# Ranking score matmuls by ScalarE's queued work in the planner of a causal attention stage

## The chip, the cores and the metric

One NeuronCore of one Trainium2 chip runs the whole program in one launch. The metric is device time in microseconds, the median of several executions. The program has six stages one after the other; the change lies in the fifth, the second attention, and there in one host-side function that writes down the order of the instructions before the kernel is built.

## The reference, cut to what matters

The program is a "macaron" of feed-forward and attention layers on 2048 tokens of width 256, each with a layer norm ahead and a residual behind:

```python
x = x + 0.5 * _L0_ffn_ref(_layernorm(x), ...)
x = x + _L0_attn_ref(_layernorm(x), ...)      # latent attention, 16 heads
x = x + 0.5 * _L0_ffn_ref(_layernorm(x), ...)
x = x + 0.5 * _L1_ffn_ref(_layernorm(x), ...)
x = x + _L1_attn_ref(_layernorm(x), ...)      # the stage of the change
x = x + 0.5 * _L1_ffn_ref(_layernorm(x), ...)
```

The second attention, with 16 heads of width 16, all 2048 tokens in one causal sequence:

```python
q, k, v = _rope(proj(Wq)), _rope(proj(Wk)), proj(Wv)
scores = jnp.einsum('bhsd,bhtd->bhst', q, k) * attn_scale
scores = jnp.where(causal, -jnp.inf, scores)
probs = jax.nn.softmax(scores, axis=-1)
out = jnp.einsum('bhst,bhtd->bhsd', probs, v)
return out.transpose(0, 2, 1, 3).reshape(B, S, E) @ Wo.T
```

The softmax is taken with the true maximum of each row, and all matmuls work on 32-bit data.

## The kernel before, in words

**Tiling.** Queries come in 4 chunks of 512 tokens and heads in 4 groups of 4; a pair (chunk j, group g) is a *unit*. There are 16 units, `UNITS` (L1327), in chunk order 0, 3, 2, 1, four units each. A unit of chunk j looks at 4(j+1) *key tiles* of 128 keys; one key tile of one unit is a *step* (160 in all). Each step has four *scores* matmuls, one for each head.

**The five kinds of TensorE work** (`attention_heads`, the TensorE block around L1800 to L1863), with what follows each on another engine:

- *maxima*: the scores of a piece of a unit with queries on the partitions, two heads at a time, into one of two PSUM `slot`s of 1024 columns. VectorE reduces the slot to row maxima (L1875, L1881) and so frees it. A unit of chunk j has 2(3+4j) such jobs: 6, 14, 22 or 30. In each half of a unit the first is a *triangle*: two bf16 matmuls with the mask on all 128 rows of the array (L1812) and eight small ones (L1816). All others are L1824. Head h uses the upper or lower 64 rows of the array, so two matmuls of different halves can run side by side.
- *turn*: when all maxima of a unit are known, VectorE combines and negates them (L1887 to L1894, event *shift*), TensorE turns them (L1831), VectorE copies them (L1900), and SyncE's queue places them beside the queries by DMA (L1790).
- *scores*: key tile against the unit's 512 queries (fewer on the diagonal: 384, 256 or 128), shift included, into one of three PSUM banks (L1841). ScalarE takes the exponential into `probs` (L1922) and so frees the bank. On the diagonal GpSimd clears what lies ahead (L1769).
- *values*: the four heads of a step against V, in four column groups of 32 (L1854; 8 matmul instructions, the 32-bit data taking two passes each). It waits until the step's four exponentials are done. `probs` holds four steps, so scores may run at most four steps ahead of values.
- *finish*: after a unit's last values, ScalarE drains the output bank (L1929), TensorE turns it back (L1861), VectorE divides (L1905, L1907).

**What sets the order.** `attention_plan` is a greedy list scheduler with a model of its own. It keeps when each slot, bank, half of the array and engine will be free (`slot_free`, `bank_free`, `half_free`, `scalar_at`, `vector_at`), works out for each kind of work that may come next the time `at` at which it could start, and takes the one with the lowest `at + PREFER[kind]`; ties go to the earlier `at`. `SWITCH` is charged where the array's layout changes (scores and maxima share "rows", values is "columns", turn and finish are "whole"), `RESULT` from a matmul to its reader, `SIGNAL` from a reader to the next writer. The result is one fixed list for each engine, which the engine's block follows in order; every instruction still waits on its semaphores. So a change of `PREFER` changes no instruction, only the order on TensorE and, where two units or kinds cross, on the other engines.

The model's charges, from the code: an exponential 0.09 + width/1200 us, a scores matmul 0.06 + width/2400, values 0.12 + width/600, a triangle 0.85, a reduction 0.1 for each part + 2 x width/960, and 4.0 us from a turn's copy until the unit's scores can start.

Before, the order comes out as a repeated pattern. Written with V for values, s for scores, m for maxima, T for turn and F for finish, the list begins `mmmmmmmmTmmmmmsssmssTsssmsmsssmsss...`; after the first four units comes `VmFmmmmmmmmmmmmmmmmmmmTmmmmmsssmss`, then long runs of `VsssmmsVsssmmsVsssmms`, and after the last maxima `VsssVsssVsss`.

Of the kernel before, what the change touches and what calls it, by code (L numbers as in the profile page):

```python
# [1328 lines left out]
HEAD_COLUMNS = D1 + 1  # L1329
PLACED = 3 * D1  # L1330
SWITCH, RESULT, SIGNAL = 0.08, 0.25, 0.12
PREFER = {"turn": -0.3, "finish": -0.3, "scores": -0.05, "maxima": 0.0, "values": 0.1}


def maxima_jobs(j):
# [21 lines left out]
def attention_plan():  # L1357
# [13 lines left out]
    mode, slot_free, bank_free = None, [0.0, 0.0], [0.0] * 3  # L1371
    step_ready, value_done = [], []
    jobs = scored = valued = unit = job = 0
    shift_at, turned, finish_at, finished, drained_at, ready_at = {}, set(), {}, set(), {-1: 0.0}, {}
    query_ready = {n: 0.0 if n < NG else 12.0 for n in range(2 * NG)}

    def wide_start(ready, to):
        return max(ready, *half_free, issue) + (0.0 if mode == to else SWITCH)

    def narrow_start(ready, halves):  # L1380
        return max(ready, issue, *(half_free[i] for i in halves)) + (0.0 if mode == "rows" else SWITCH)

    while scored < GROUP * len(steps) or valued < len(steps) or len(finished) < units:
        choices = []
        free = slot_free[jobs % 2]
        for n in sorted(shift_at):
            if n not in turned:
                choices.append((wide_start(max(free, shift_at[n]), "whole"), PREFER["turn"], "turn", n))
        for n in sorted(finish_at):
            if n not in finished:  # L1390
                choices.append((wide_start(max(free, finish_at[n]), "whole"), PREFER["finish"], "finish", n))
        if unit in query_ready:
            choices.append((narrow_start(max(free, query_ready[unit]), (0, 1)), PREFER["maxima"], "maxima", unit))
        if scored < GROUP * len(steps):
            step, h = divmod(scored, GROUP)
            n, kt = steps[step]
            if n in ready_at and (step < PROB_STEPS or len(value_done) > step - PROB_STEPS):
                choices.append((narrow_start(max(bank_free[scored % 3], ready_at[n]), (h % 2,)), PREFER["scores"], "scores", n))
        if valued < len(step_ready):
            n, kt = steps[valued]  # L1400
            if n - 1 in drained_at:
                choices.append((wide_start(max(step_ready[valued], drained_at[n - 1] if kt == 0 else 0.0), "columns"),
                                PREFER["values"], "values", n))
        _, at, kind, n = min((c[0] + c[1], c[0], c[2], c[3]) for c in choices)
# [29 lines left out]
        elif kind == "scores":  # L1434
            step, h = divmod(scored, GROUP)
# [7 lines left out]
            scalar_at = start + 0.09 + width / 1200  # L1443
# [11 lines left out]
        elif kind == "values":  # L1455
# [5 lines left out]
            if kt == key_tiles(j) - 1:  # L1461
                scalar_at = max(scalar_at, end + RESULT)
# [248 lines left out]
def attention_heads(core, scratch, first_query, key, v_one, attended):  # L1711

    nc = core.nc
    plan = attention_plan()
    ring = {e[2]: e for e in plan["tensor"] if e[0] in ("maxima", "turn", "finish")}
    place = {(e[0], e[1]): e[2] for e in plan["tensor"] if e[0] in ("turn", "finish")}
# [284 lines left out]
```

How the kernel before makes its waits and increments, by code:

```python
    def __call__(self, instruction):  # L133
        instruction.then_inc(self.sem, 1)
        self.n += 1
        self.engine.wait_ge(self.sem, self.n)
# [26 lines left out]
    def vector(self, dve):  # L163
        dve.wait_ge(self.masks_loaded, 16)
        self.core.nc.vector.tensor_copy(self.core.masks[:], self.masks[:]).then_inc(self.masks_ready, 1)
# [19 lines left out]
    def vector(self, dve):  # L186
        for b in range(0, 2 * NCH, 2):
            dve.wait_ge(self.turned, b + 1)
            self.core.nc.vector.tensor_copy(self.place(b), self.banks[b % len(self.banks)][:]).then_inc(self.evac_dve, 1)
# [1 line left out]
    def scalar(self, act):  # L191
        for b in range(1, 2 * NCH, 2):
            act.wait_ge(self.turned, b + 1)
            self.core.nc.scalar.activation(self.place(b), self.banks[b % len(self.banks)][:], ACT.Copy).then_inc(self.evac_act, 1)
# [1 line left out]
    def tensor(self, pe):  # L196
        nc, n = self.core.nc, len(self.banks)
        for b in range(2 * NCH):
            c, d = divmod(b, ND)
            if self.source_ready is not None:
                pe.wait_ge(self.source_ready, TPC * (c + 1))
            if b >= n:
                pe.wait_ge(self.evac_act if b % 2 else self.evac_dve, (b - n) // 2 + 1)
            for i in range(TPC):
                last = nc.tensor.transpose(self.banks[b % n][:, i * P:(i + 1) * P],
                                           self.source[:, TPC * c + i, d * P:(d + 1) * P], self.core.ident)
            last.then_inc(self.turned, 1)
```

## Time and profile before

| | |
|---|---|
| median of 3 runs | 1953.37 us (1953.34 to 1963.35) |
| the profiled execution, its own time | 1954.15 us |
| its span, first to last instruction | 1952.4 us |
| TensorE busy | 1731.2 us, 89% |
| VectorE busy | 1529.0 us, 78% |
| ScalarE busy | 1179.7 us, 60% |
| GpSimd busy | 983.2 us, 50% |
| mean granted TensorE clock | 0.933 |

"Busy" is the union of the durations of an engine's instructions; matmuls are pipelined, so a busy TensorE need not be at its peak. Granted clock 1 is 2.4 GHz and 0.5 is 1.2 GHz; a value between is a stretch with both. The stage of the change runs from about 1432 to 1896 us of the span.

### The profile page before, as it was taken

How to read it: one execution, taken by the hardware profiler on the slowest of the kernel's cores; microseconds unless marked ns; L12 is line 12 of the kernel's file. 1: busy time of each engine (PE TensorE's matmuls, PEld its weight loads, DVE VectorE, ACT ScalarE, POOL GpSimd, SP SyncE). 2: the span in 40 equal slices, each digit the busy share in tenths (PEclk: the TensorE clock that was granted, in tenths of full speed). 3: DMA queues.
4: the chain of work that ended last, by engine and by line, in shares of the span. 5: the costliest groups of instructions: out<-in, count | busy, mean ns of one | idle time of the engine just before them, and what ended most of it. 6: DMA issues, size and time to landing. Idle time of an engine off the chain costs nothing. (4 is left out here: it accounts for less than half of the span.)

```text
span 1952.4 us, 27188 instructions
## 1 busy us (share of the span) xinstructions
PE 1731.2 (89%) x9368; PEld 1005.0 (51%) x9368; DVE 1529.0 (78%) x2236; ACT 1179.7 (60%) x2043; POOL 983.2 (50%) x820
## 2 busy tenths in 40 slices
PE   4667899999999999999999997557978999999996
PEld 3544555555555565565555653456644444444445
DVE  6763888998898888988889887776658888887716
ACT  1145787776876777777778774111323577777760
POOL 0004798897896988979879886011401000010110
PEclk8786999999999999999999999677968899999988
DMA  3200000000000000000000000111430200200001
GB/s 100 63 16 24 1 1 1 15 1 15 1 1 15 1 6 10 1 15 1 0 7 1 1 1 3 45 46 38 97 55 2 33 2 2 34 2 2 2 2 43
DMA packets 26697, 34.34 MB, mean 18 GB/s; under 512 B 5312, under 2 KB 19648, under 8 KB 26432
## 3 DMA queue, kind: packets, MB, share of 16 engines
q1 hardware_dynamic: 25360, 31.28, 6.7%
q8 instruction: 76, 1.25, 0.3%
q10 hardware_dynamic: 1200, 1.31, 0.2%
q14 instruction: 61, 0.50, 0.1%
HBM read 26.03 MB, written 6.29 MB: 17 GB/s over the span
## 5 line engine op out<-in xcount | busy, mean ns | idle before, releaser
L1208 POOL TENSOR_TENSOR lath_summed<-lath_summed,lath_held 128x512 f32<-128x512 f32 x392 | 524.8, 1339 | 54.4 <-ACT lath_held L1114 27.5
L1922 ACT ACTIVATE atth_probs<-atth_score 128x512 f32<-128x512 f32 (+3 forms) x640 | 293.3, 542 | 156.4 <-PE atth_score L1841 154.1
L1279 DVE TENSOR_TENSOR lath_held<-lath_held,lath_shift 128x1024 f32<-128x1024 f32 (+2 forms) x352 | 331.2, 968 | 24.6 <-PE lath_shift L1027 15.0
L1108 ACT ACTIVATE lath_held<-lath_score 128x1024 f32<-128x1024 f32 (+2 forms) x352 | 283.7, 828 | 105.1 <-DVE lath_largest L1232 51.5
L1881 DVE TENSOR_REDUCE atth_maxima<-atth_slot 128x2 f32<-128x1024 f32 (+3 forms) x288 | 285.9, 1041 | 53.5 <-PE atth_slot L1824 52.5
L1114 ACT ACTIVATE lath_held<-lath_held 128x1024 f32<-128x1024 f32 (+2 forms) x352 | 292.6, 861 | 48.7 <-DVE lath_held L1279 47.1
L1014 PE MATMUL lath_out<-lath_held,lat_latent 128*64 128x512 f32 (+1 forms) x1152 | 302.9, 591 | 8.0 <-ACT lath_held L1114 4.3
L998 PE MATMUL lath_score<-lath_query_hi,lat_key_hi 128*128 128x512 f32 x576 | 246.7, 428 | 22.8 <-ACT lath_held L1108 17.7
L1769 POOL TENSOR_SCALAR_AFFINE_SELECT atth_probs<-atth_probs 128x512 f32<-128x512 f32 x64 | 40.6, 635 | 433.9 <-ACT atth_probs L1922 433.9
L1003 PE MATMUL lath_score<-lath_query_hi,lat_key_lo 128*128 128x512 f32 x576 | 231.0, 401 | 0.0
L1232 DVE TENSOR_TENSOR lath_largest<-lath_score,lath_largest 128x1024 f32<-128x1024 f32 (+2 forms) x240 | 211.5, 881 | 17.6 <-PE lath_score L1003 12.6
L999 PE MATMUL lath_score<-lath_query_lo,lat_key_hi 128*128 128x512 f32 x576 | 219.8, 382 | 0.0
L998 PEld LDWEIGHTS lath_score<-lath_query_hi,lat_key_hi 128*128 128x128 f32 x576 | 108.8, 189 | 155.1 <-issue 80.7
L1214 POOL TENSOR_TENSOR lath_turn_a<-lath_query,lat_rope 128x512 f32<-128x512 f32 x64 | 86.4, 1350 | 190.5 <-DVE lath_turn_b L1285 155.7
L1854 PE MATMUL atth_out<-atth_probs,att_v_one 128*32 128x512 f32 (+3 forms) x1280 | 154.3, 556 | 0.6 <-POOL atth_probs L1769 0.5
L1003 PEld LDWEIGHTS lath_score<-lath_query_hi,lat_key_lo 128*128 128x128 f32 x576 | 110.4, 192 | 19.8
L1841 PE MATMUL atth_score<-atth_query,att_key 50*128 50x512 f32 (+3 forms) x384 | 116.4, 457 | 1.7 <-ACT atth_probs L1922 1.1
L999 PEld LDWEIGHTS lath_score<-lath_query_lo,lat_key_hi 128*128 128x128 f32 x576 | 109.3, 190 | 14.5
L1014 PEld LDWEIGHTS lath_out<-lath_held,lat_latent 128*64 128x64 f32 x1152 | 61.8, 135 | 92.4 <-issue 69.4
L1285 DVE TENSOR_TENSOR lath_turn_b<-lath_turn_b,lat_rope 64x512 f32<-64x512 f32 x64 | 76.7, 1199 | 31.1 <-ACT lath_turn_b L1141 29.5
L1841 PEld LDWEIGHTS atth_score<-atth_query,att_key 50*128 50x128 f32 x384 | 52.0, 190 | 92.3 <-ACT atth_probs L1922 86.2
L1224 POOL TENSOR_TENSOR lath_query_lo<-lath_query,lath_query_hi 128x512 fp32r<-128x512 f32 x64 | 83.7, 1308 | 15.3 <-ACT lath_query_hi L1148 15.3
(345 smaller groups left out, 2920.6 us busy)
## 6 DMA issues: line engine op xcount, KB each, us to landing
att_first_query<-att_scratch SPq DMA_DIRECT2D x12, 256.0 KB, 9.1
atth_query<-att_scratch SPq DMA_DIRECT2D x12, 256.0 KB, 8.9
ffn_a_w<-in_L_ffn_W SPq DMA_DIRECT2D x2, 1024.0 KB
lat_raw_out<-in_L_attn_w_out SPq DMA_DIRECT2D x8, 256.0 KB, 2.7
lat_rope<-in_c_rope_feature SPq DMA_DIRECT2D x1, 2048.0 KB, 10.8
ffn_b_w<-in_L_ffn_W SPq DMA_DIRECT2D x2, 1024.0 KB, 7.1
mix_a_factors<-in_L_ffn_factors SPq DMA_DIRECT2D x8, 256.0 KB, 4.3
att_scratch<-attp_high SPq DMA_DIRECT2D x4, 512.0 KB, 2.8
```

What stands on the lines that cost most here:

```text
L998: nc.tensor.matmul(scores, key_hi[:, keys], hi, start=True, stop=False)
L999: nc.tensor.matmul(scores, key_hi[:, keys], lo, start=False, stop=False)
L1003: last = nc.tensor.matmul(scores, key_lo[:, keys], hi, start=False, stop=True)
L1014: last = nc.tensor.matmul(by_head(out_bank[KL * i:KL * i + KL, :], q0), latent[:, kt, 0:KL], by_head(slot(n)[:, i, :], q0), start=(step == ...
L1108: nc.scalar.activation(part_columns(slot(n), tiles, q0), part_columns(score_bank[n % 2], tiles, q0), ACT.Copy)\
L1114: nc.scalar.activation(columns, columns, ACT.Exp, scale=SCALE0)\
L1208: nc.gpsimd.tensor_tensor(total, total, slot(n)[:, i, :], ALU.add).then_inc(s["tiles_summed"], 1)
L1232: nc.vector.tensor_tensor(out, first, second, ALU.max).then_inc(s["maxed"], 1)
L1279: nc.vector.tensor_tensor(columns, columns, added, ALU.subtract)\
L1841: nc.tensor.matmul(score_bank[u % 3][:, q0:CH], key_rows(GROUP * g + h, PLACED + 2, kt * P, P), query_rows(n, h, PLACED + 2, q0, CH - q0), ...
L1881: nc.vector.reduce_max(maxima[:, n % 2, :, pair, i, at], slot[r % 2][:, :, begin:begin + width], AX.X)\
L1922: nc.scalar.activation(probs[:, step % PROB_STEPS, h, q0:CH], score_bank[u % 3][:, q0:CH], ACT.Exp, scale=SCALE1)\
```

## The change

The constants of preference are moved, and the preference of scores is no longer constant: it grows with the work that ScalarE would still have in front of it 0.5 us (`RESULT * 2`) after the matmul could start.

```diff
-PREFER = {"turn": -0.3, "finish": -0.3, "scores": -0.05, "maxima": 0.0, "values": 0.1}
+PREFER = {"turn": -0.2, "finish": -0.2, "scores": 0.0, "maxima": 0.0, "values": 0.05}
+SCORES_PER_LAG, LAG_LIMIT = 0.1, 1.7
 
@@ attention_plan
             if n in ready_at and (step < PROB_STEPS or len(value_done) > step - PROB_STEPS):
-                choices.append((narrow_start(max(bank_free[scored % 3], ready_at[n]), (h % 2,)), PREFER["scores"], "scores", n))
+                at = narrow_start(max(bank_free[scored % 3], ready_at[n]), (h % 2,))
+                queued = min(max(scalar_at - at - RESULT * 2, -LAG_LIMIT), LAG_LIMIT)
+                choices.append((at, PREFER["scores"] + SCORES_PER_LAG * queued, "scores", n))
```

Nothing else changes: the same instructions, tiles, semaphores and transfers.

## Rows read from the trace of the kernel before

**Rows 1.** Cores: span and mean granted clock.

```profile
core 0: 1952.4 us, clock 0.933
```

**Rows 2.** Windows: stretch, length, busy by engine (instructions), granted clock, DMA share, GB/s.

```profile
0.00:1432.40 1432.40, 1250.06 (x6280) 778.00 (x6280) 1150.36 (x1739) 872.86 (x1376) 942.58 (x756) 0.94 0.06 19
1432.40:1453.00 20.60, 14.98 (x77) 8.25 (x79) 13.70 (x25) 1.28 (x1) 0.00 (x0) 0.53 0.65 78
1453.00:1492.00 39.00, 38.51 (x289) 19.61 (x288) 27.78 (x43) 24.83 (x67) 10.15 (x16) 0.86 0.01 2
1492.00:1523.50 31.50, 21.57 (x85) 9.44 (x83) 28.90 (x34) 0.60 (x1) 0.00 (x0) 0.55 0.00 1
1523.50:1852.50 329.00, 326.68 (x2212) 140.50 (x2212) 271.01 (x308) 243.42 (x517) 24.69 (x39) 0.99 0.09 11
1852.50:1895.80 43.30, 40.26 (x245) 14.39 (x241) 3.73 (x11) 30.40 (x71) 5.79 (x10) 0.86 0.01 1
```

**Rows 3.** Waits of VectorE, 1453 to 1492: total us, times, longest.

```profile
DVE atth_maxima L1875 <- PE atth_slot L1816: 7.4, 5, 2.1
DVE atth_maxima L1881 <- PE atth_slot L1824: 4.2, 5, 1.1
```

**Rows 4.** Waits of ScalarE, then of VectorE, 1529 to 1852.5.

```profile
ACT atth_probs L1922 <- PE atth_score L1841: 82.4, 114, 3.0
...
DVE atth_maxima L1881 <- PE atth_slot L1824: 46.4, 69, 2.4
DVE atth_maxima L1875 <- PE atth_slot L1816: 7.9, 13, 1.6
```

**Rows 5.** Timeline of one step with four scores: start, us, engine, instructions.

```profile
1583.94 1.06 PE L1854 MATMUL atth_out<-atth_probs,att_v_one 128*32 128x512 f32 x8
1584.93 0.72 PE L1841 MATMUL atth_score<-atth_query,att_key 50*128 50x512 f32 x3
1585.28 0.85 PE L1824 MATMUL atth_slot<-att_key,atth_query 48*128 48x512 f32 x4
1586.12 0.49 PE L1841 MATMUL atth_score<-atth_query,att_key 50*128 50x512 f32 x1
1586.54 0.64 PE L1854 MATMUL atth_out<-atth_probs,att_v_one 128*32 128x512 f32 x4
...
1585.46 1.58 ACT L1922 ACTIVATE atth_probs<-atth_score 128x512 f32<-128x512 f32 x3 [0.54 <-PE atth_score L1841]
...
1585.93 1.23 DVE L1881 TENSOR_REDUCE atth_maxima<-atth_slot 128x2 f32<-128x1024 f32 x1 [0.89 <-PE atth_slot L1824]
```

**Rows 6.** Timeline, TensorE: a step with three scores, one with five.

```profile
1597.93 1.06 PE L1854 MATMUL atth_out<-atth_probs,att_v_one 128*32 128x512 f32 x8
...
1599.77 0.64 PE L1854 MATMUL atth_out<-atth_probs,att_v_one 128*32 128x512 f32 x4
...
1592.23 1.07 PE L1854 MATMUL atth_out<-atth_probs,att_v_one 128*32 128x512 f32 x8
...
1595.33 0.64 PE L1854 MATMUL atth_out<-atth_probs,att_v_one 128*32 128x512 f32 x4
```

**Rows 7.** Timeline, TensorE and then VectorE, early in the stage.

```profile
1456.78 0.58 PE L1841 MATMUL atth_score<-att_first_query,att_key 50*128 50x256 f32 x1
1457.29 1.03 PE L1812 MATMUL atth_slot<-masks 128*128 128x512 bf16 x2
...
1459.41 1.23 DVE L1875 TENSOR_REDUCE atth_maxima<-atth_slot 128x8 f32<-128x1024 f32 x1 [1.84 <-PE atth_slot L1816]
```

**Rows 8.** Timeline, TensorE: a step that ends with a triangle.

```profile
1777.57 1.06 PE L1854 MATMUL atth_out<-atth_probs,att_v_one 128*32 128x512 f32 x8
...
1779.42 0.38 PE L1841 MATMUL atth_score<-att_first_query,att_key 50*128 50x256 f32 x1
1779.73 0.61 PE L1812 MATMUL atth_slot<-masks 128*128 128x512 bf16 x2
1780.27 0.66 PE L1816 MATMUL atth_slot<-att_key,atth_query 48*128 48x128 f32 x8
1780.86 0.64 PE L1854 MATMUL atth_out<-atth_probs,att_v_one 128*32 128x512 f32 x4
```

**Rows 9.** Timeline, TensorE, at the low clock after the last maxima.

```profile
1861.82 1.91 PE L1854 MATMUL atth_out<-atth_probs,att_v_one 128*32 128x512 f32 x8
```

## The prediction

> **What bounds the kernel now.** I began with the cores [rows 1], to have the span and the clock, and then cut the span with the windows view at the places where the stage of the change alters its character [rows 2]. The reader is to see five stretches there. The 1432 us ahead of the stage are untouched. From 1432 to 1453 only the first maxima run. From 1453 to 1492 the four small units of chunk 0 go through: VectorE is busy 27.78 of 39 us. From 1492 to 1523.5 VectorE is busy 28.90 of 31.5 us while ScalarE does 0.60: the first unit of chunk 3 needs 30 maxima before a single one of its scores may go, and nothing else is left. This stretch is bound by VectorE. From 1523.5 to 1852.5 TensorE shows 326.68 of 329 us, VectorE 271.01 and ScalarE 243.42; after it the maxima are over and the last 43 us are scores and values alone.
>
> Second, the waits. In the long stretch ScalarE still waits 82.4 us for scores and VectorE 54 us for slots to be filled [rows 4], so neither is the bound; TensorE's order is. Third, the timeline of one common step, `VsssmmsV` [rows 5]. It takes 1586.54 - 1583.94 = 2.60 us and is a chain of latencies: values start at 0 and hold the array until the first score at +1.00 (rounded from 0.99); its exponential starts at +1.52, 0.54 us of ScalarE idle; the three exponentials take 1.58 us together, so about 0.5 us from start to start; the first frees its bank at about +2.1, the fourth score follows at +2.18, and the next values at +2.60, 0.42 us after it. Of the 132 steps that start between 1529 and 1852, 71 have four scores, 25 three and 16 five (counted from the planner's list of before, laid beside the trace). The two others have their price in [rows 6]: three scores 1599.77 - 1597.93 = 1.84 us, five 1595.33 - 1592.23 = 3.10 us. A pair of three and five is thus 4.94 us against 5.20 us for two fours, 0.26 us cheaper.
>
> **The change part by part.** It removes and adds no instruction, no wait and no transfer. What it moves is worked out by stepping through the planner's rule, with the states that the list of before gives.
>
> *Scores against maxima.* Before, scores led by 0.05 always. Now they lead by 0.1 x (-queued). After values, ScalarE has run dry: queued is about -0.48, scores lead by 0.048, and the first score goes first as before. For the second, queued is 0.52, but maxima need both halves and could start 0.26 later, so it too stays. The third has queued 0.78: it costs its start + 0.078, and maxima could start 0.02 later at + 0. Before, the score won by 0.03; now maxima win by 0.06. The step becomes `VssmsmsV`, with the third score behind one maxima job. Stepped through three periods, this pattern repeats with four scores, two maxima and a period of 2.57 in the model, as before.
>
> What does that cost on the chip? In [rows 5] the third score is one half-array matmul of about 0.2 us beside the first maxima. Behind it, its result arrives about 0.2 us later, near +2.1; ScalarE wants it only after two exponentials, at +1.52 + 1.0 = +2.5. The cover is those two queued exponentials; if it is gone, the price is 0.2 us a step. The fourth score still waits for the first exponential, so the chain of 2.60 stays whole: **0 us**. VectorE gets its first slot about 0.2 us earlier, and it idles 0.89 us before it in [rows 5], so most of that is not needed.
>
> *The triangle* is the exception. It is a maxima job that fills the array: in [rows 8] it runs from 1779.73 to the next values at 1780.86, 1.13 us, where the plan charges 0.85. If it is put ahead of the third score, that result comes near +1.33 + 1.13 + 0.5 = +2.96 instead of +2.5: ScalarE is dry for 0.46 us. There are 24 triangles behind chunk 0; but the fourth score is not ready much before, and next to the values that follow the triangle takes its time in either order. I take 0, with bounds 0 and 24 x 0.46 = 11 us of loss.
>
> *Values against scores.* Values stood 0.15 behind; now 0.05 - 0.1 x queued, about 0.01 at a queue of 0.41. By hand, after the fourth score the values now win by 0.06 where they won by 0.02, so some five-score steps become four, and their three-score partners with them. All 16 lost would cost 16 x 0.26 = 4.2 us. But where a slot is not yet free after the third score, values now step in sooner (0.01 decides), which makes new three-score steps, and these must be paid back with five or more, because scores and values are fixed in number. If 35 pairs of the 71 fours became three and five it would gain 9.1 us. I take 0, since both shifts are of the same size; bounds +4.2 and -9.1.
>
> A rule speaks here. The Trainium skill ("TensorEngine Tiling (Array Packing)", Key Properties) says that changing the tiling mode, not merely the tile, drains the array. By that rule alone the price would follow the number of mode changes, which is nearly fixed (160 values groups), and a three-five pair would be worth nothing; this case's trace agrees that a change costs something, with the 0.42 us from score to values above, and differs in that the pair is worth 0.26 us.
>
> *The early stretch.* From 1453 to 1492 VectorE waits 7.4 + 4.2 = 11.6 us for slots [rows 3], and whatever is saved there moves the whole VectorE-bound stretch and all after it. [Rows 7] is such a wait: a score starts at 1456.78, the triangle behind it at 1457.29, and VectorE had been idle 1.84 us. With the triangle ahead, it comes 0.51 us sooner. The states with queued 0.78 and maxima 0.02 behind occur four times there, once for each unit: 4 x 0.51 = **-2.0 us**. Bounds: 0 (the slot was what it waited for) and -11.6 (every wait gone).
>
> *Turn and finish* lose 0.1 against maxima and about 0.05 + 0.04 against waiting scores. The one turn that matters is the first of chunk 3, ahead of which ScalarE is dry: there it stood at 78.18 - 0.3 against maxima at 78.10; with 0.2 it is 77.98 and still first: 0. Had it flipped, one reduction of 1.23 us [rows 5] would be added. The DMAs of each turn, and the query loads behind them on SyncE's queue, move with the turn; they are issued several us before their scores, so 0. GpSimd follows the exponentials and covers itself.
>
> *After the last maxima* the choice is between scores and values only. A few third scores fall behind values. Bounds: one step of values either way, which at the low clock takes 1.84 us to the next score (1.91 busy [rows 9]); taken 0.
>
> Sum: -2.0 + 0 + 0 + 0. The profiled execution took 1954.15 us (its span 1952.4 and 1.75 around it); -2.0 gives 1952.15. The median of the runs shown lies 0.8 below that execution, so the forecast for the median is **1951.4 us**.
>
> **The rivals.**
>
> *Faster, by a better mix.* The rule feeds VectorE and TensorE while ScalarE is full. For it: TensorE's order binds, and 11.6 and 54 us of VectorE's waits are there to be had. If half of the early waits go (-5.8) and 20 pairs form (-5.2), the time is 1953.4 - 11 = 1942 us. Against it: the chain of 2.60 us does not shorten by reordering inside a step.
>
> *Slower, by maxima ahead of scores.* One mechanism: TensorE takes its list in order, so maxima ranked ahead of the third score put it behind a 1.13 us triangle, or behind a slot that VectorE has not freed. In the plan a triangle costs 0.28 us too little, so it will not see this. With 24 triangles at 0.46 us the time is 1953.4 + 11 - 2 = 1962.4 us; with the 4.2 us of lost pairs 1966.6. It decides from about 22 triangles so placed and nothing gained early (22 x 0.46 = 10). Against it: most of the 24 already stand behind the third score by the slot's own time.
>
> *The order hardly changes where it counts.* The model ties are broken by 0.01 to 0.06, and slot times may keep the old order in most steps; then 1953 us, not to be told from the forecast by time, but by the order.
>
> **How the numbers follow.** About 0.5% (9.8 us) is what a measurement of this kernel can tell from no change. The forecast, with its own range of about 1945 to 1958, has 0.55; no real change of order 0.10; the faster rival 0.22; the slower one 0.13. The range takes in the forecast and most of both rivals: low 1941, which is the faster rival and a little of its bounds, and high 1961, most of the triangles' bound. The chances are 0.22 faster, 0.65 within 0.5%, 0.13 slower.
>
> **What would show each step.** In the changed timeline, a full step should read values, two scores, maxima, score, maxima, score and last 2.60 us; ScalarE's idle after values should stay 0.54. VectorE's waits from 1453 to 1492 should fall from 11.6 to about 9.6, and the first exponential of chunk 3, now at the end of the VectorE-bound stretch near 1524, should come about 2 us sooner. ScalarE's 82.4 us of waits in the long stretch should stay within 5 us. Steps of 3.3 us that hold a triangle between the second and third score, with ScalarE idle twice, would show the slower rival; more steps of 1.8 and 3.1 us with fewer of 2.6 would show the faster. The prediction is wrong if the long stretch, 329 us now, changes by more than 8 us.

## The result, and the profile after

The median of four runs is **1936.77 us** (1931.35 to 1940.07), against 1957.96 us for four runs of the kernel before in the same comparison: ratio 0.9877, 95% interval 0.9848 to 0.9907. The change is faster by 1.2%, and ends below the predicted range of 1941 to 1961 us. Four executions below were in a slower state of the chip (2071.35 us of e1, 2424.97 us of the kernel before, 1968.35 and 1974.78 us of e12): the medians hold them, the ratios and the times at equal clock do not. The two profiled executions took 1954.15 and 1940.07 us at nearly the same mean granted clock, so their traces can be laid side by side.

The cores and the windows of the kernel after, cut where the stage alters its character (columns as in [rows 2]; lines of this kernel stand 3 further down than before):

```profile
core 0: 1938.3 us, clock 0.932
```

```profile
0.00:1433.60 1433.60, 1252.35 (x6280) 781.64 (x6280) 1151.77 (x1739) 873.22 (x1376) 942.57 (x756) 0.94 0.06 19
1433.60:1454.00 20.40, 14.52 (x77) 7.89 (x79) 13.62 (x24) 1.28 (x1) 0.00 (x0) 0.54 0.66 79
1454.00:1497.50 43.50, 43.37 (x291) 21.51 (x293) 27.90 (x43) 25.08 (x67) 10.15 (x16) 0.75 0.01 2
1497.50:1527.50 30.00, 20.13 (x81) 8.55 (x81) 28.55 (x34) 0.60 (x1) 0.00 (x0) 0.60 0.01 1
1527.50:1839.00 311.50, 310.73 (x2197) 135.25 (x2197) 270.90 (x307) 242.81 (x512) 23.48 (x37) 0.99 0.09 12
1839.00:1882.00 43.00, 38.03 (x260) 14.41 (x256) 4.74 (x12) 31.99 (x76) 6.98 (x11) 1.00 0.01 1
```

Against [rows 2], the stretch before the stage is 1.2 us longer, the four small units of chunk 0 take 43.5 us for 39, at a granted clock of 0.75 for 0.86, and the VectorE-bound stretch is 1.5 us shorter. The whole gain stands in one row: the long stretch is **311.5 us for 329**, with the same work in it (VectorE 270.90 for 271.01 us, ScalarE 242.81 for 243.42) and the same clock of 0.99. So 17.5 us of waits went. Which ones, the waits of the two consumers there say (total us, times, longest), to be read against [rows 4]:

```profile
ACT atth_probs L1925 <- PE atth_score L1844: 96.6, 127, 30.2
DVE atth_maxima L1884 <- PE atth_slot L1827: 34.1, 68, 1.8
DVE atth_maxima L1878 <- PE atth_slot L1819: 3.0, 6, 1.1
```

ScalarE's total holds the 30.2 us ahead of chunk 3, which the window of [rows 4] leaves out: without it 66.4 us for 82.4. VectorE waits 37.1 us for 54.3. Early in the stage, by contrast, nothing was saved; from 1453 to 1492 its two waits are these, 12.2 us for the 11.6 of [rows 3]:

```profile
DVE atth_maxima L1878 <- PE atth_slot L1819: 6.9, 5, 3.1
DVE atth_maxima L1884 <- PE atth_slot L1827: 5.3, 4, 2.3
```

**The common step.** TensorE and ScalarE, one full-width step after, as [rows 5] of before:

```profile
1546.87 1.06 PE L1857 MATMUL atth_out<-atth_probs,att_v_one 128*32 128x512 f32 x8
1547.86 0.50 PE L1844 MATMUL atth_score<-atth_query,att_key 50*128 50x512 f32 x2
1548.20 0.39 PE L1827 MATMUL atth_slot<-att_key,atth_query 48*128 48x512 f32 x2
1548.43 0.39 PE L1844 MATMUL atth_score<-atth_query,att_key 50*128 50x512 f32 x1
1548.45 0.60 PE L1827 MATMUL atth_slot<-att_key,atth_query 48*128 48x512 f32 x2
1549.04 0.50 PE L1844 MATMUL atth_score<-atth_query,att_key 50*128 50x512 f32 x1
1549.47 1.07 PE L1857 MATMUL atth_out<-atth_probs,att_v_one 128*32 128x512 f32 x8
```

```profile
1548.39 2.06 ACT L1925 ACTIVATE atth_probs<-atth_score 128x512 f32<-128x512 f32 x4 [0.54 <-PE atth_score L1844]
```

Values, two scores, maxima, score, maxima, score: the order worked out, in 1549.47 - 1546.87 = 2.60 us, with 0.54 us of ScalarE idle. Nothing is gained here. From 1529 to 1852.5 us 50 groups of values are followed by four scores; 27 of them read like this one (2.57 us on average), and 19 read `VssmmssV` (2.62 us).

**The end of a unit.** In the last four steps of a unit, those on the diagonal, the scores are 512, 384, 256 and 128 wide. Here are the last of unit 6 and the first of unit 7, TensorE before, and under it ScalarE:

```profile
1643.72 1.07 PE L1854 MATMUL atth_out<-atth_probs,att_v_one 128*32 128x512 f32 x8
...
1645.89 1.07 PE L1854 MATMUL atth_out<-atth_probs,att_v_one 128*32 128x512 f32 x8
1646.88 0.44 PE L1841 MATMUL atth_score<-atth_query,att_key 50*128 50x128 f32 x3
1647.05 0.66 PE L1824 MATMUL atth_slot<-att_key,att_first_query 48*128 48x256 f32 x4
1647.58 0.32 PE L1841 MATMUL atth_score<-atth_query,att_key 50*128 50x128 f32 x1
1647.83 1.07 PE L1854 MATMUL atth_out<-atth_probs,att_v_one 128*32 128x512 f32 x8
1648.83 0.50 PE L1824 MATMUL atth_slot<-att_key,att_first_query 48*128 48x512 f32 x2
1649.26 0.85 PE L1854 MATMUL atth_out<-atth_probs,att_v_one 128*32 128x384 f32 x8
1650.04 0.50 PE L1824 MATMUL atth_slot<-att_key,att_first_query 48*128 48x512 f32 x2
1650.37 0.64 PE L1841 MATMUL atth_score<-atth_query,att_key 50*128 50x512 f32 x3
```

```profile
1645.14 1.24 ACT L1922 ACTIVATE atth_probs<-atth_score 128x256 f32<-128x256 f32 x4 [1.10 <-PE atth_score L1841]
1647.25 0.97 ACT L1922 ACTIVATE atth_probs<-atth_score 128x128 f32<-128x128 f32 x4 [0.87 <-PE atth_score L1841]
1650.81 4.04 ACT L1922 ACTIVATE atth_probs<-atth_score 128x512 f32<-128x512 f32 x8 [2.60 <-PE atth_score L1841]
```

Four exponentials 128 wide last 0.97 us and cannot cover a group of values of 1.07; then two groups, each with maxima behind it, go ahead of the next unit's first score, and ScalarE is dry for 2.60 us. The same place after:

```profile
1644.69 1.06 PE L1857 MATMUL atth_out<-atth_probs,att_v_one 128*32 128x512 f32 x8
...
1646.67 0.47 PE L1844 MATMUL atth_score<-atth_query,att_key 50*128 50x128 f32 x2
1647.07 0.85 PE L1857 MATMUL atth_out<-atth_probs,att_v_one 128*32 128x384 f32 x8
1647.85 0.61 PE L1844 MATMUL atth_score<-atth_query,att_key 50*128 50x128 f32 x3
...
1648.54 0.66 PE L1844 MATMUL atth_score<-atth_query,att_key 50*128 50x512 f32 x2
...
1649.63 0.86 PE L1857 MATMUL atth_out<-atth_probs,att_v_one 128*32 128x256 f32 x16
```

```profile
1646.11 1.35 ACT L1925 ACTIVATE atth_probs<-atth_score 128x256 f32<-128x256 f32 x5 [0.64 <-PE atth_score L1844]
1648.21 2.44 ACT L1925 ACTIVATE atth_probs<-atth_score 128x128 f32<-128x128 f32 x6 [0.76 <-PE atth_score L1844]
```

(The last row's run of six ends with 512-wide ones.) The largest wait is 0.76 us, and the last two groups of values, one 256 and one 128 wide, go back to back, 0.86 us for both, while ScalarE works on the next unit's wide scores.

Laying the planner's list beside the traces, I summed this over units 4 to 11. "Full" is the time from a unit's first score to its first diagonal one, "ends" from there to the next unit's first score. The last two rows come from the planner alone.

```
                                  before   after
full                               207.8   210.2 us
ends                                83.1    66.2 us
groups of values in the ends          36      28
ScalarE waits of 0.75 us or more      30       9  (37.9 and 9.1 us; the wait before chunk 3 left out)
maxima jobs in the ends               60      51
scores ahead of values, mean        2.67    1.44  (finished steps, counted at each score)
scores barred by the ring             98       8  (decisions of the planner in units 4 to 15; in 4 to 11: 82 and 3)
```

"Barred by the ring" means that a score could not be chosen because the values of four steps earlier (`PROB_STEPS`) were not yet planned. **The ends lose 16.9 us and the full-width part gains 2.4.** More than the whole 14.1 us by which the two spans differ thus lies in 32 of the 112 score steps of these units. The ends also hold 9 maxima jobs fewer; no run moved those by themselves.

The clock has no part in most of this. From the first score of unit 5 to that of unit 12 both kernels were granted 1.00 throughout, and the stretch takes 236.45 us for 248.37: 11.9 us less. Before, and under it after:

```profile
1566.40:1814.80 248.40, 246.69 (x1686) 105.33 (x1684) 206.87 (x235) 184.60 (x391) 17.78 (x28) 1.00 0.06 8
```

```profile
1568.10:1804.50 236.40, 235.83 (x1682) 101.76 (x1682) 205.31 (x233) 185.64 (x393) 18.28 (x29) 1.00 0.06 8
```

The trace of the changed kernel run once more (e16) has 236.45 us there again.

### The profile page after: what moved, and what is told of

It reads as the page before. It is cut to its first block and busy times, and to the rows that moved or that the text cites. A ratio compares the mean times of both kernels' runs of the same rounds, so it can differ in the third digit from the quotient of the medians.

```text
span 1938.3 us, 27188 instructions
## 1 busy us (share of the span) xinstructions
PE 1717.4 (89%) x9368; PEld 1003.3 (52%) x9368; DVE 1531.0 (79%) x2236; ACT 1181.3 (61%) x2043; POOL 983.2 (51%) x820
## 5 line engine op out<-in xcount | busy, mean ns | idle before, releaser
L1114 ACT ACTIVATE lath_held<-lath_held 128x1024 f32<-128x1024 f32 (+2 forms) x352 | 292.6, 861 | 50.3 <-DVE lath_held L1279 48.6
L998 PE MATMUL lath_score<-lath_query_hi,lat_key_hi 128*128 128x512 f32 x576 | 246.8, 428 | 22.4 <-ACT lath_held L1108 17.2
L1232 DVE TENSOR_TENSOR lath_largest<-lath_score,lath_largest 128x1024 f32<-128x1024 f32 (+2 forms) x240 | 211.7, 882 | 17.5 <-PE lath_score L1003 12.5
L1844 PEld LDWEIGHTS atth_score<-atth_query,att_key 50*128 50x128 f32 x384 | 51.9, 187 | 90.7 <-ACT atth_probs L1925 82.8
L1224 POOL TENSOR_TENSOR lath_query_lo<-lath_query,lath_query_hi 128x512 fp32r<-128x512 f32 x64 | 84.2, 1316 | 14.9 <-ACT lath_query_hi L1148 14.9
```

The source lines that it names most:

```text
L998: nc.tensor.matmul(scores, key_hi[:, keys], hi, start=True, stop=False)
L1114: nc.scalar.activation(columns, columns, ACT.Exp, scale=SCALE0)\
L1232: nc.vector.tensor_tensor(out, first, second, ALU.max).then_inc(s["maxed"], 1)
L1844: nc.tensor.matmul(score_bank[u % 3][:, q0:CH], key_rows(GROUP * g + h, PLACED + 2, kt * P, P), query_rows(n, h, PLACED + 2, q0, CH - q0), ...
```

## The experiments

Raw ratios are to the kernel before of the same comparison. The mean granted clock varied from one execution to the next (0.917 to 0.934 for the kernel before), and the time with it: 12.6 us for 0.01 over 100 executions of the kernel before, 12.4 pooled over all kernels here. Where less than 1% matters I therefore also give the time **at a clock of 0.930**, each execution corrected by that slope (standard errors 0.2 to 1.2 us). Before stands at 1956.4, the changed kernel at 1941.5 (4 executions) and, run once more, 1939.8 (5). The correction takes for granted that the clock causes the time and not the order the clock; e9 below shows why that matters.

### First four: constants of values and the order inside a step

The accounts were: the number of times that TensorE enters values sets the time (account E), and the third score's place inside a step does (O).

**e1**, the change with the old preference of values (and of turn and finish, which e6 tests alone).

```diff
-PREFER = {"turn": -0.2, "finish": -0.2, "scores": 0.0, "maxima": 0.0, "values": 0.05}
+PREFER = {"turn": -0.3, "finish": -0.3, "scores": 0.0, "maxima": 0.0, "values": 0.1}
```

> The changed kernel with three constants of the old table: turn and finish -0.3 and values 0.1; the term for ScalarE's queue stays, scores stay at 0.0. In its list TensorE goes to values 158 separate times (157 before the change, 146 after it), while maxima stand ahead of the third score as after the change (93 steps begin Vssm, 90 after, 27 before). Theory E (entries: what the change gains is fewer separate entries to values, at about 14 us / 11 = 1.3 us each): ratio to before 0.997 to 1.003. Theory O (order inside the step: maxima ahead of the third score feed VectorE sooner): ratio 0.987 to 0.992, as the whole change.

Measured: 1950.85 us, 0.9933 [0.9905, 0.9961]; at equal clock 1949.5, 6.9 below before. That lies between the two ranges, so neither account had it. There are 158 entries to values, for 157 before and 146 after, and 78.7 us of ends with 33 groups in them. The queue term by itself gives under half of the gain, with the entries unchanged.

**e2**, before, values moved forward all the way.

```diff
-PREFER = {"turn": -0.3, "finish": -0.3, "scores": -0.05, "maxima": 0.0, "values": 0.1}
+PREFER = {"turn": -0.3, "finish": -0.3, "scores": -0.05, "maxima": 0.0, "values": 0.0}
```

> The kernel of before with one constant changed, values 0.1 to 0.0, and no term for the queue. TensorE goes to values 133 separate times instead of 157, and the third score stays ahead of maxima (93 steps begin Vsss, 2 begin Vssm). Theory E: 24 entries fewer at about 1.3 us, so some 30 us less if each were worth as much, ratio 0.982 to 0.990. Theory O: ratio 0.998 to 1.005, since nothing in the order that it counts on is changed.

1980.98 us, 1.0066 [1.0032, 1.01]; at equal clock 1964.9, +8.5. It has 133 entries, 24 fewer than before, and is slower: **account E falls**.

**e3** and **e4** alter only the finished list, at 60 and 84 places.

```diff
+    order = plan["tensor"]
+    for i in range(len(order) - 5):
+        if [e[0] for e in order[i:i + 5]] == ["values", "scores", "scores", "maxima", "scores"]:
+            order[i + 3], order[i + 4] = order[i + 4], order[i + 3]
```

> The changed kernel, where in TensorE's list alone the third score and the maxima job ahead of it change places in the 60 steps that begin Vssms (they become Vsssm); everything else as after the change, 146 entries to values. Theory E: as the changed kernel, within 0.2% of it, ratio to before 0.986 to 0.990. Theory O: two thirds of the gain are lost, ratio 0.995 to 0.998.

> The kernel of before, where in TensorE's list alone the third score goes behind the first maxima job in the 84 steps that begin Vsssm (they become Vssms); 157 entries to values as before. Theory E: ratio to before 0.998 to 1.002. Theory O: ratio 0.987 to 0.993.

e3 (the edit shown, on the changed kernel): 1944.04 us, 0.9896 [0.9872, 0.992], at equal clock 1941.7. e4 (the opposite exchange on before): 1964.11 us, 0.9997 [0.9966, 1.0027], at equal clock 1955.7. Neither moves by more than 1.9 us, and the full-width part of e3 is 210.8 us for 210.2. **O falls**, and the prediction's 0 us for this step holds.

### Next four: constants and the ring

Account P: scores run up against the ring of four steps, and the change frees them from it.

**e5**, before with values at 0.05.

```diff
-PREFER = {"turn": -0.3, "finish": -0.3, "scores": -0.05, "maxima": 0.0, "values": 0.1}
+PREFER = {"turn": -0.3, "finish": -0.3, "scores": -0.05, "maxima": 0.0, "values": 0.05}
```

> The kernel of before with one constant changed: values 0.1 to 0.05. Theory P (probs ring: before, values stood so far behind scores that scores ran the full four steps ahead, and then were barred until values had been done, which starves ScalarE for 1 to 3 us at the ends of units): the planner bars a score in 98 of its decisions behind chunk 0 before the change, 8 after it, and 22 here. So most of the change's 15 us at equal clock are expected from this constant alone: 8 to 13 us less than before at equal clock. Theory E (count of entries to values, 153 here against 157): 5 us less. Rival Q (the term for ScalarE's queue is what gains): within 3 us of before.

1975.48 us, 1.008 [1.0048, 1.0112]; at equal clock 1963.0, +6.6, where P expected 8 to 13 us less. Only 22 scores are barred, for 98, yet the ends grew to 96.4 us with 39 groups; two of the eight took 17.2 and 14.9 us, and nine times in the plan no score could go because the next unit wasn't ready.

**e6**, the change with the old turn and finish.

```diff
-PREFER = {"turn": -0.2, "finish": -0.2, "scores": 0.0, "maxima": 0.0, "values": 0.05}
+PREFER = {"turn": -0.3, "finish": -0.3, "scores": 0.0, "maxima": 0.0, "values": 0.05}
```

> The changed kernel with turn and finish back at -0.3. No score is barred in the plan (0 decisions), 147 entries. Theory P and theory E: as the changed kernel, within 3 us at equal clock. If turn and finish at -0.2 carried a part of the gain, it shows here as a loss of more than 3 us.

1938.84 us, 0.9894 [0.9855, 0.9933]; at equal clock 1941.0. Nothing, as predicted; so e1's loss is that of values alone.

**e7** and **e8** change the ring.

```diff
-PROB_STEPS = 4
+PROB_STEPS = 3
```

> The changed kernel with a probs ring of three steps instead of four (the planner plans for it too; it bars a score in 7 decisions, 147 entries). Theory P: the changed order runs 1.4 steps ahead on average and has no use for the fourth step, so the time stays within 3 us of the changed kernel at equal clock. A rival by which a deep ring hides latencies on the chip that the plan does not know: 5 us or more slower.

> The kernel of before with a probs ring of five steps instead of four (65 barred decisions instead of 98, scores 3.05 steps ahead on average instead of 2.80, 153 entries). Theory P: a third of the barred decisions gone, so 3 to 7 us less than before at equal clock, by fewer starvations of ScalarE over 1 us. Without theory P: no change.

e7 (the edit shown, on the changed kernel): 1941.57 us, 0.9903 [0.987, 0.9937], at equal clock 1941.5, the same as with four. e8 (before with five): 1962.55 us, 1.0027 [1.0003, 1.0051], at equal clock 1958.2, +1.8, where P expected 3 to 7 us less. With five steps the planner of before still meets its end 65 times and leaves 41 groups for the ends. Space alone isn't the cause; the changed order doesn't even need the fourth step.

### Third four: the ring another way, the table alone, the charges

Account Q: the queue term by itself makes the gain. Theory T, as the expectations call it: two causes add up, scores barred by the ring at the ends of units and VectorE fed too late.

**e9**, before, where values lose their handicap once scores are three steps ahead.

```diff
-                                PREFER["values"], "values", n))
+                                PREFER["values"] if scored // GROUP - valued < 3 else 0.0, "values", n))
```

> The kernel of before with one line changed: values keep their 0.1 while scores are under three steps ahead of them, and get 0.0 from three steps on. The plan then bars a score for want of a probs slot in 5 decisions instead of 98. No term for the queue. Theory T (two causes: before, ScalarE is starved at the ends of units where scores are barred by the ring, which costs about half of the 15 us; the other half is VectorE fed too late, which the queue term mends): 3 to 7 us less than before at equal clock, most of it between the first scores of units 8 and 12 (123.5 us before; 117 to 121 here), the stretch of units 4 to 7 less so. If barring alone were the cause, all 15 us; if it were none, no change.

1972.31 us, 1.0053 [1.0027, 1.0079]; at equal clock 1954.5, -1.9, where T expected 3 to 7 us less. Only 5 scores are barred, and next to nothing is gained over the whole program: **P alone falls** as the cause of the 15 us. Part of it is there: units 8 to 11, at a granted clock of 1.00 in both traces, take 119.4 us for 123.5, as expected. But the twelve executions of e9 had a mean clock of 0.9175 (0.913 to 0.926), the 29 of the kernel before beside them 0.926 (0.917 to 0.934). In its trace the wide part of unit 4 was granted 0.68 and that of unit 7 0.81, for 0.86 and 1.00 before. The executions of e5 and e11 were also granted less than those beside them (0.9185 and 0.9197 for 0.927 and 0.926). So an order may bear on the clock, and a time at equal clock may leave out a part of what the order does.

**e10**, the same line on e1, so queue term and relief together with values at 0.1.

> The line of e9_ring_relief and the queue term together, on the table turn and finish -0.3, scores 0.0, maxima 0.0, values 0.1 (that is e1_values_back with the ring relief). 156 separate entries to values, as before the change; 2 barred decisions. Theory T: both causes mended by another way than the change's table, so 10 to 14 us less than before at equal clock. Theory E (entries counted): no gain over e1's 7 us.

1953.81 us, 0.9949 [0.9927, 0.9972]; at equal clock 1944.8, -11.6. That lies between e1 (-6.9) and the changed kernel (-15 to -16.5), with 29 groups in the ends and 70.6 us, and within what T expected. Two parts of -6.9 and -1.9 give -11.6 together; with standard errors of 1.2, 0.6 and 0.7 us that is not clearly more than their sum.

**e11**, the new table without the queue term.

```diff
-SCORES_PER_LAG, LAG_LIMIT = 0.1, 1.7
+SCORES_PER_LAG, LAG_LIMIT = 0.0, 1.7
```

> The changed kernel with the queue's weight at 0.0 instead of 0.1: the new table alone. 0 barred decisions, 124 separate entries. Theory T: values and scores now both crowd out maxima, VectorE is fed late and the next unit's scores are not ready when the last ones end, so 8 to 20 us slower than before at equal clock. Theory E and a theory of barring alone: faster than the changed kernel.

1987.44 us, 1.0134 [1.0101, 1.0166]; at equal clock 1974.0, +17.6, as T expected. Its timeline, TensorE and ScalarE, shows what the steps look like:

```profile
1540.27 1.07 PE L1857 MATMUL atth_out<-atth_probs,att_v_one 128*32 128x512 f32 x8
1541.26 0.50 PE L1827 MATMUL atth_slot<-att_key,atth_query 48*128 48x512 f32 x2
1541.69 0.60 PE L1815 MATMUL atth_slot<-masks 128*128 128x512 bf16 x2
1542.22 0.66 PE L1819 MATMUL atth_slot<-att_key,atth_query 48*128 48x128 f32 x8
1542.72 0.68 PE L1844 MATMUL atth_score<-atth_query,att_key 50*128 50x512 f32 x3
```

```profile
1539.19 2.06 ACT L1925 ACTIVATE atth_probs<-atth_score 128x512 f32<-128x512 f32 x4 [2.29 <-PE atth_score L1844]
1543.21 2.07 ACT L1925 ACTIVATE atth_probs<-atth_score 128x512 f32<-128x512 f32 x4 [1.95 <-PE atth_score L1844]
```

Scores and maxima both stand at 0 now, so maxima, even a triangle, go directly behind values, and the next score comes 1542.72 - 1540.27 = 2.45 us after them for 0.99 before. In units 4 to 11 maxima follow 71 of 110 groups of values directly, for 6 of 109 after the change. So one job of the queue term is to put back, when ScalarE is dry, the lead that the table's -0.05 gave. What it adds is that this lead is gone when ScalarE is full. Q falls too, since e1 has the term and gains 6.9 us only.

**e12**, all charges set nearer to what the traces show, with a table to go with them.

```diff
-SWITCH, RESULT, SIGNAL = 0.08, 0.25, 0.12
-PREFER = {"turn": -0.2, "finish": -0.2, "scores": 0.0, "maxima": 0.0, "values": 0.05}
-SCORES_PER_LAG, LAG_LIMIT = 0.1, 1.7
+SWITCH, RESULT, SIGNAL = 0.056, 0.583, 0.135
+PREFER = {"turn": -0.278, "finish": -0.368, "scores": -0.041, "maxima": 0, "values": 0.164}
+SCORES_PER_LAG, LAG_LIMIT = 0.137, 0.399
...
-                queued = min(max(scalar_at - at - RESULT * 2, -LAG_LIMIT), LAG_LIMIT)
+                queued = min(max(scalar_at - at - 0.579, -LAG_LIMIT), LAG_LIMIT)
...
-            end = at + (0.85 if what == "triangle" else 0.04 + 0.03 * len(parts) + width / 2400)
+            end = at + (0.956 if what == "triangle" else 0.04 + 0.03 * len(parts) + width / 2400)
...
-            end = at + 0.12 + (CH - queries_from(kt, j)) / 600
+            end = at + 0.176 + (CH - queries_from(kt, j)) / 600
```

> The changed kernel's planner with charges nearer to what the traces show (RESULT 0.583 for 0.25, triangle 0.956 for 0.85, values 0.176 for 0.12 fixed, SWITCH 0.056, SIGNAL 0.135) and a table to go with them (turn -0.278, finish -0.368, scores -0.041, values 0.164, weight 0.137, limit 0.399, queue counted from 0.579 us). 158 entries, 11 barred decisions, 88 steps with three scores and 27 with six where the changed kernel has 45 and 23. Theory T, with the prices of steps in the trace of before (two of three and one of six come cheaper than three of four): 5 to 10 us less than the changed kernel at equal clock. If the changed kernel is at the bound: the same.

1949.91 us, 0.9941 [0.9911, 0.9971]; at equal clock 1939.1, no better than the changed kernel's 1939.8 to 1941.5: a miss. As a ratio it is even 0.6% behind, since its mean clock was 0.922. The execution of e12 whose trace was kept is the one of 1968.35 us at a clock of 0.909, so its trace says little of the order. Not one of the kernels here beats the changed one.

### Last four: where the gain comes from

Account D: a group of values costs little beside 512-wide exponentials and much in the narrow ends, so that the gain is the 8 groups that left the ends. Account J: full width and ends act only together, since what is done in one part decides how far ahead the other begins.

**e13**, the changed list, with one group of each of units 4 to 10 put from the wide part into the third step of the end, which is 256 wide (seven groups).

```diff
+    done = [e for e in order if e[0] == "values"]
+    for unit in range(4, 11):
+        width = TPC * UNITS[unit][0]
+        begin, narrow, third = (next(i for i, e in enumerate(order) if e[0] == "scores" and e[1] == unit and e[2] == kt and e[3] == h)
+                                for kt, h in ((0, 0), (width, 0), (width + 2, 3)))
+        taken = [i for i in range(begin, narrow) if order[i][0] == "values"][-2]
+        order.insert(third, order.pop(taken))
+    for i, e in zip([i for i, e in enumerate(order) if e[0] == "values"], done):
+        order[i] = e
```

> The changed kernel, where in TensorE's list alone one group of values in each of units 4 to 10 is taken out of the full-width steps and put among the narrow steps at the unit's end (35 groups of values run there in units 4 to 11 instead of 28; 36 before the change). Theory D (the change gains because fewer values are left to do among the short exponentials at the ends of units; over the runs so far 8 groups fewer go with 17 us less there, 2 us each): 10 to 16 us slower than the changed kernel at equal clock. If the groups of values only go along with the real cause: 0 to 5 us.

1957.29 us, 0.9981 [0.9956, 1.0006]; at equal clock 1949.5, 8.0 above the changed kernel's first runs and 9.7 above its second. The ends hold 35 groups again and take 80.3 us. That is 8 to 9.7 us for 7 groups, **1.1 to 1.4 us each**, with planner, constants and all other work as they were. It lies under D's range of 10 to 16 us and above its rival's of 0 to 5, so D holds in part. Not all of the 80.3 us is due to the groups: 9.0 of the 14.1 us by which these ends are longer than the changed kernel's lie in those of units 6 and 7, which the traced execution ran at a granted clock of 0.60 and 0.74, for 1.00. Units 5, 8, 9 and 10, at 1.00 in both traces, are 0.4, 0.8, 1.1 and 1.2 us longer as a whole. Unit 11, from which no group was moved, takes 29.9 us in both.

**e14** has the new table and term only while the next score is one of a full-width part, **e15** only while it is one of an end.

```diff
+OLD = {"turn": -0.3, "finish": -0.3, "scores": -0.05, "maxima": 0.0, "values": 0.1}
+NEW = {"turn": -0.2, "finish": -0.2, "scores": 0.0, "maxima": 0.0, "values": 0.05}
...
+        here, tile = steps[min(scored // GROUP, len(steps) - 1)]
+        PREFER, SCORES_PER_LAG = (NEW, 0.1) if tile < TPC * UNITS[here][0] else (OLD, 0.0)
```

> The changed planner's table and queue term only while the next score is one of a full-width step; the old table for the narrow steps. 30 groups of values and 50 maxima jobs at the ends of units 4 to 11 (28 and 51 after the change, 36 and 60 before it). Theory D: most of the gain is there, 9 to 15 us less than before at equal clock. Rival J (both places must act together): 4 to 7 us less.

> The reverse: the changed table and queue term only while the next score is one of a narrow step, the old table for full width. 37 groups of values and 59 maxima jobs at the ends, as many as before. Theory D: 0 to 3 us less than before at equal clock. Rival J: 4 to 7 us less.

e14 (shown): 1954.51 us, 0.9972 [0.9944, 1.0], at equal clock 1950.0, -6.4. e15 (`tile >=`): 1953.97 us, 0.9969 [0.9946, 0.9993], at equal clock 1952.0, -4.4. Both lie where J expected them. Their sum is -10.8, against -15 to -16.5 for the whole: J holds in part, since each gives something by itself and 4 to 6 us come only with both. e14 also shows the limit of D: 30 groups and 50 maxima jobs in its ends, nearly as few as after the change, and still 78.1 us there. Two of its ends were granted 0.77 and 0.82; the six at 1.00 take 57.4 us, for 48.6 after the change and 62.1 before.

**e16**, the changed kernel once more beside these three.

> The changed kernel itself, in the same rounds as the others: 13 to 17 us less than before at equal mean clock; the ratio of the medians 0.985 to 0.992, because the mean granted clock of an execution moves its time by some 12 us for each 0.01 and differs from run to run. All theories.

1937.44 us, 0.9895 [0.9857, 0.9933]; the first result, 0.9877, comes again.

## Why the prediction was wrong

**Right** were the terms of the full-width step. The order `VssmsmsV` came as stepped and kept 2.60 us and 0.54 us of idle; the third score's place is worth nothing (e3, e4); turn and finish are worth nothing (e6); the slower rival didn't come, as of the four waits of 1.0 us or more that ScalarE has in units 4 to 11 (the one before chunk 3 left out, the largest 1.73) none has a triangle ahead of its score. The rival of an unchanged order was refuted by the trace.

**The early stretch** was given -2.0 us and came out +3.0 us to the first score of chunk 3 (94.3 for 91.3 us from the stage's begin). VectorE's waits were to fall from 11.6 to 9.6 and are 12.2. The profiled execution had a granted clock of 0.75 there for 0.86, which hides what the order does. The trace of e6 shows it: its list up to there is the changed one but for one turn that goes one score sooner, and it was granted 0.87. Its window from 1453 to 1492, and VectorE's waits there:

```profile
1453.00:1492.00 39.00, 38.73 (x293) 19.23 (x291) 28.17 (x44) 25.31 (x68) 10.15 (x16) 0.87 0.01 2
```

```profile
DVE atth_maxima L1878 <- PE atth_slot L1819: 5.3, 5, 1.8
DVE atth_maxima L1884 <- PE atth_slot L1827: 4.2, 5, 1.4
```

They come to 9.5 us, as forecast, but the first score of chunk 3 comes 90.7 us after the stage's begin, 0.6 us sooner than before and not 2.0. So the fall of the waits was forecast rightly; that all of it would reach the end of the stretch was not.

**The step that failed is "Values against scores", taken as 0** between +4.2 and -9.1. The long stretch changed by 17.5 us, where more than 8 was named as the refutation. I priced values by full-width steps alone, where losing or winning a pair is worth 0.26 us, and never stepped through the last three tiles of a unit. The true term was about -15 at equal clock, beyond the bound of -9.1: -16.9 in the ends and +2.4 in the full-width part of the profiled pair. The working rested on "both shifts are of the same size". In the full-width part the two nearly cancel in time; at the ends they do not, where an exponential of 128 columns lasts 0.97 / 4 = 0.24 us for the 0.53 of a wide one, while a group of values beside it still takes 1.07 us. The working also took the number of changes to values and back as nearly fixed; it went from 157 to 146, and it does not order the times (133 entries 1964.9 us in e2, 146 entries 1954.5 in e9 and 1941.5 after the change). From 1529 to 1852.5 us there are 124 groups of values and not 132, which alters nothing, since the counts of 71, 25 and 16 are right.

**The faster rival** had the sign and about the size (1942), but not the mechanism: it wanted half of the early waits and 20 pairs of three and five. The early waits fell by 2.1 us at most (e6). The mix did move, but otherwise: in the full-width parts of units 4 to 11, 44 groups of values with four scores behind them became 38, 13 with three 18, 9 with five 5, 2 with six 12, and 7 groups follow another directly. These parts together got no shorter (210.2 us for 207.8, with 81 groups in them for 73).

**What took its place**, as far as shown. (1) The gain is in the ends: the traces. (2) Moving seven groups of values back there costs 8 to 9.7 us at equal mean clock, and 0.4 to 1.2 us each where the clock was 1.00: e13. (3) No constant does it alone: table without term +17.6, term without the table's values -6.9, values at 0.05 without term +6.6, rule in one part -6.4 and -4.4. The reading, not tested by itself, is that a weaker handicap of values keeps scores 1.4 steps ahead instead of 2.7, so a unit's end begins with few values owed, and that the queue term is what makes the weaker handicap harmless, because a dry ScalarE still gets its score first. **Open** are how the rest, a third of the gain or more, divides between fewer maxima jobs in the ends and a better place for each piece of work (e14 has few of both and dear ends), and how much of the raw 1.2% is the clock: 15 to 16.5 us (0.8%) are left at equal clock, which from 1953.4 us ends at 1937 to 1938, below the range as well, and units 5 to 11 alone give 11.9 us at a clock of 1.00 in both.

## What to carry to other kernels

When a planner's rule changes, step through it by hand not only at the commonest step but wherever tiles get narrow or a unit ends: what hides behind a long instruction is bare behind a short one. List the idle gaps of the consumer by size, and look at what precedes the largest: here 30 waits of 0.75 us or more held 37.9 us that no common step showed. Constants of a greedy rule act jointly, so that half of such a change may be slower than none (e11, e5); test them in pairs before calling one useless. Where a gain is smaller than what the granted clock does to the time, look for a stretch that both traces ran at the same clock, and compare that.

## What the runs showed of the hardware

The mean granted clock of executions of one program on one core spread from 0.917 to 0.934 for the kernel before, and its time from 1971.2 to 1950.2 us with it, about 12.4 us for 0.01. An order's gain of 0.8% is smaller than that spread.

The spread can sit in one place of the trace. e4's list differs from that of the kernel before in the order inside some steps only, and at equal clock the two kernels agree (1955.7 and 1956.4 us). But its traced execution (1969.97 us, for 1954.15) ran the small units of chunk 0 at a granted clock of 0.50. Before, and under it e4:

```profile
1453.00:1495.00 42.00, 40.18 (x303) 20.47 (x301) 30.78 (x46) 25.43 (x68) 10.15 (x16) 0.87 0.01 2
```

```profile
1453.00:1495.00 42.00, 41.95 (x209) 21.12 (x209) 20.26 (x34) 19.36 (x51) 7.66 (x12) 0.50 0.01 2
```

The first score of chunk 3 came 108.7 us after the stage's begin, for 91.3. Those 17.4 us are more than the 15.8 by which the two executions differ. Where the clock is 1.00, executions of one list agree closely: units 5 to 11 of the changed kernel took 236.45 us twice.

Two groups of values back to back, 256 and 128 wide, took 0.86 us together (the row at 1649.63 us), while a group 512 wide holds back the next score by 0.99 us, and the next values come 0.42 us after the last score [rows 5]. A ring of three steps of exponentials did as well as one of four (e7), and five were no better (e8).
